# Update passes: where VectorE does the second and the third head's scan and product around the edge layer norm

## What is computed

```python
for i in range(L):                       # L = 3, H = 4 heads, dh = 16
    q, k, v = h @ Wq[i], h @ Wk[i], h @ Wv[i]      # per head
    scores = einsum('ehd,ehd->eh', q[dst], k[src]) / sqrt(dh)
    scores = scores + e @ We[i]
    p = exp(scores - segment_max(scores, dst)[dst])
    alpha = p / (segment_sum(p, dst)[dst] + 1e-09)
    agg = segment_sum(alpha[:, :, None] * v[src], dst)
    h = ln(h + agg @ Wo[i])
    emsg = gelu(concat([h[src], h[dst], e]) @ Wem[i] + bem[i])
    e = ln(e + emsg)                     # 32 features an edge
```

## Time and profile before

| | us |
|---|---|
| median of 3 runs | 10914.1 (10911.99 to 10914.28) |
| profiled execution | 10918.62 |
| its span, first to last instruction | 10916.8 |
| VectorE busy in the span | 6547.4 (60%) |
| POOL busy | 8001.4 (73%) |
| PE busy | 5191.6 (48%) |
| ScalarE busy | 4657.7 (43%) |

### The profile page before, as it was taken

The page is one execution under the profiler, slowest core; times in us unless marked ns, Lnnn a source line. Parts: engine busy times, 40 slices in busy tenths (PEclk is TensorE's granted clock), DMA queues, the critical chain, the costliest instruction groups (busy, mean ns, idle before and its releaser), DMA issues. The chain is left out here.

```text
span 10916.8 us, 87549 instructions
## 1 busy us (share of the span) xinstructions
PE 5191.6 (48%) x22037; PEld 4373.7 (40%) x22037; DVE 6547.4 (60%) x11572; ACT 4657.7 (43%) x5207; POOL 8001.4 (73%) x7864
## 2 busy tenths in 40 slices
PE   5344426885885786688588400011111433343333
PEld 5333425774774676577477300011111322232222
DVE  6333325664665566566466555554555688858887
ACT  0010004664664665566466322223333455535553
POOL 7888885776776776777677677767776777757774
PEclk8555556996997898799699655555555566656665
DMA  5333333332332232233254333333443555535553
GB/s 191 34 34 38 34 21 87 81 82 49 83 79 64 67 81 72 58 81 82 62 135 129 103 113 120 121 92 126 133 131 110 162 176 183 176 116 177 184 175 103
DMA packets 693316, 1131.52 MB, mean 104 GB/s; under 512 B 403255, under 2 KB 468070, under 8 KB 685558
## 3 DMA queue, kind: packets, MB, share of 16 engines
q0 software_dynamic: 364224, 383.74, 18.7%
q1 hardware_dynamic: 265088, 397.86, 11.4%
q10 hardware_dynamic: 63926, 349.09, 8.1%
HBM read 674.29 MB, written 468.68 MB: 105 GB/s over the span
## 5 line engine op out<-in xcount | busy, mean ns | idle before, releaser
L877 POOL DMA_INDIRECT turned<-d_t,idx x6076 | 5749.1, 946 | 1921.6 <-issue 1851.3
L1032 PE MATMUL banks<-pair,hot 128*128 128x462 f32 x13720 | 3177.7, 395 | 680.0 <-DVE wide L1127 586.0
L1032 PEld LDWEIGHTS banks<-pair,hot 128*128 128x128 f32 x13720 | 2759.3, 203 | 1097.5 <-DVE wide L1127 678.3
L648 POOL DMA_INDIRECT d_acc<-work,idx x784 | 1237.9, 1579 | 252.0 <-issue 234.4
L1237 DVE COPY idx<-src 128x28 int32 x252 | 45.8, 182 | 1871.5 <-DMA turned<-d_t,idx 1868.8
L1325 DVE TENSOR_TENSOR_SCAN wide<-banks,wide 128x224 f32<-128x224 f32 (+1 forms) x1008 | 1023.7, 1077 | 6.0 <-DVE wide L1319 0.3
L930 ACT ACTIVATE hot<-wide,row 128x896 fp32r<-128x896 f32 x980 | 930.1, 1030 | 77.7 <-DMA wide<-d_key 48.9
L1064 PE MATMUL banks<-ident,wide 128*128 128x128 f32 x588 | 162.0, 421 | 1681.3 <-ACT wide L897 863.2
L1305 DVE TENSOR_TENSOR wide<-turned,banks 128x1792 f32<-128x1792 f32 x252 | 860.3, 3414 | 0.0
L1003 ACT COPY wide<-wide 128x924 f32<-128x924 f32 (+1 forms) x252 | 477.2, 1894 | 873.2 <-DVE wide L1325 869.3
L1064 PEld LDWEIGHTS banks<-ident,wide 128*128 128x128 f32 x588 | 102.3, 211 | 1748.8 <-ACT wide L897 894.4
(11 more groups left out here) (295 smaller groups left out, 8308.5 us busy)
## 6 DMA issues: line engine op xcount, KB each, us to landing
d_e<-wide ACTq DMA_DIRECT2D x168, 924.0 KB
turned<-d_t,idx POOLq DMA_INDIRECT x6076
d_e<-wide ACTq DMA_DIRECT2D x84, 1008.0 KB
wide<-d_b SPq DMA_DIRECT2D x60, 1344.0 KB
wide<-d_key SPq DMA_DIRECT2D x145, 448.0 KB, 3.7
wide<-d_b SPq DMA_DIRECT2D x60, 896.0 KB, 4.6
d_b<-wide SPq DMA_DIRECT2D x28, 1344.0 KB
wide<-d_edge SPq DMA_DIRECT2D x84, 448.0 KB, 5.3
```

The costliest lines, as they stand in the source:

```text
L648: gp.indirect_dma_start(g.d_acc[r][:, :], offset(idx[:, b, k:k + 1]), sums[:, b, k, :], None, compute_op=ALU.add).then_inc(added[b][r], 16)
L877: gp.indirect_dma_start(rows[:, b, k, :], None, table[:, :], offset(idx[:, b, k:k + 1])).then_inc(s["gathered"][b], 16)
L1032: mm = nc.tensor.matmul(ps_cols[i], hot[:, place, i, j, :], flat(g.pair[:, part, j]), start=(j, part) == (0, 0), stop=(j, part) == (SETS - ...
```

## The change

In update passes, the scan and product of head 2 and the product of head 1 change their places among VectorE's instructions:

- before the layer norm stood product 0, scan 1, product 1, scan 2; now product 0, scan 1
- in the wait for ScalarE's squares stood product 2; now product 1
- behind the layer norm stood scan 3, product 3; now scan 2, product 2, scan 3, product 3.

```diff
@@ -1240,15 +1240,13 @@
                 e = e_rows[:, b]
                 link(product_q(G, 0))
                 link(spread_q(b, 1))
-                link(product_q(G, 1))
-                link(spread_q(b, 2))
                 v.wait_ge(s["gelu_done"], chunk + 1)
                 v.wait_ge(s["e_loaded"][b], 16 * (t + 1))
                 link(nc.vector.tensor_tensor(norm, norm, e, ALU.add))
                 link(nc.vector.tensor_reduce(stat[:, 0], norm, AX.X, ALU.add))
                 nc.vector.scalar_tensor_tensor(norm, bc(stat[:, 0], DE), -1.0 / DE, norm,
                                                ALU.mult, ALU.add).then_inc(s["centred"], 1)
-                link(product_q(G, 2))
+                link(product_q(G, 1))
                 v.wait_ge(s["squared"], chunk + 1)
                 link(nc.vector.tensor_reduce(stat[:, 1], sq[:], AX.X, ALU.add))
...
@@ -1264,7 +1262,7 @@
             else:
-                for i in range(0 if not update else 3, NH):
+                for i in range(0 if not update else 2, NH):
                     if i:
                         spread = spread_q(b, i)
                         if i == NH - 1:
```

## The result

| | before | after |
|---|---|---|
| median of the runs, us | 10914.1 (10910.6 to 10914.7) | 10855.5 (10854.4 to 10858.7) |
| profiled execution, us | 10918.62 | 10855.53 |
| its span, us | 10916.8 | 10853.6 |
| mean granted clock of TensorE | 0.688 | 0.691 |

The ratio is 0.9948, with a 95% interval from 0.9934 to 0.9962: 58.6 us less, where 54 were forecast. In the listing of after the lines of the update pass stand two lower: L1245 is the norm's first add (before L1247), L1258 the new e, L1285 the addition to the logits, L1303 the weighting of v.

What follows compares the result with a forecast made beforehand. VectorE's work before the norm set its start, the gelu lying ready 1.42 or 0.86 us. Twice 27.9 is 55.8, less 2 for gathers: 54 off 10918.62 gives 10864.6; the median's 4.5 lower gives 10860, range 10842 to 10880.

Steps and rivals of the forecast that it cites:

- The wait at L1287 is cover, and the gelu is the limit: Update chunks: L1287's wait covers the moved 1.92 us, falling from 149.8 to about 42; gelu ready only 1.42 or 0.86 early.
- 13 x 1.32 + 14 x 0.76 a pass: Front of the norm: gain per chunk of each kind after a 0.1 us hand-over; with 0.1 for chunk 0, 27.9 us.
- The gathers at the start of a pass: Chunk 3 of the second pass: late gathers lose about 1.1 us once; 2 us taken for both passes, between 0 and 6.
- POOL: Gathers need 35.06 us a chunk against 35.4: POOL stops waiting in most chunks, stays behind for some 18 each pass.
- 0.3 us to spare behind the new e: Before L1287: VectorE ready 15.1 us after t, L1287 at t + 15.40 in the quickest chunks, so all moved work is covered.
- The squares' wait: Sum behind the squares: product of head 1 replaces that of head 2, same shape, 0.44 us stays open, nothing changes.
- The table load: Ahead of the gelu: rows give 2.21 us from L1005; the skill's drain would give 2.66, some 12 us less gain.
- (a): Rival, TensorE's clock at the We product: all chunks slow 10869, all quick 10842; chance 0.82 together with the forecast.
- (b): Rival: the gelu waits for PE's sums (L1082) at the low clock, 41 us of gain lost, 10901; chance 0.05.
- (c): Rival, no gain: a wait the trace does not show eats the 1 us a chunk, 10914; chance 0.07.
- (d): Rival, slower: gathers' landing decides above 9.5 us, makes it slower above 11.5; 10921, or 10948 with one more; chance 0.05.
- (e): Rival: the whole 1.92 us a chunk taken from in front of the norm is won, 10807; chance 0.01.

Runs made afterwards that it cites:

- scan-only kernel: Against the changed kernel, the product of head 1 went back in front of the norm, nothing filling the squares' wait: 10855.86 us, ratio 0.9948.
- pair on one chip: The changed kernel and the kernel before, each run again unchanged with a profile on the same chip: 10858.24 us and 10912.74 us.
- more work behind the new e: Against the changed kernel, scan 1 went into the wait for the squares and product 1 behind the new e: 10858.66 us, ratio 0.9951.
- before with ReLU: The kernel before with ReLU in place of the edge gelu, results not the reference's: 14158.88 us, ratio to before 1.0012.
- all eight kernels: ReLU in before and in the changed kernel; on the changed kernel gelu early twice, exponentials early twice, both, both with 26 gathers: 13876.36 to 14158.88 us.
- kernels with the exponentials early: Changed kernel with ScalarE's message-row copy (L912) and store moved behind the exponentials: 14097.79 and 14004.84 us; with the gelu early too: 14026.92.
- early gelu: Changed kernel with the next chunk's gelu issued between ScalarE's two state copies: 14141.04 us and again 14060.24, ratios 0.9998 and 0.9988 to before.
- two gathers fewer: Changed kernel with gelu and exponentials early, POOL gathering 26 of 28 columns, results not the reference's: 13876.36 us, ratio 0.9861 to before.

## Why the prediction was right

**The wait at L1287 is cover, and the gelu is the limit.** Right. The wait ends at t + 16.02 whatever VectorE does, before and after, and went from 149.8 to 41.6 us, with 42 forecast. The chunk lost 1.0 us and not the 1.92 that left the front. The scan-only kernel shows it most directly: 1.25 us taken out of the front do as much as 1.92.

**13 x 1.32 + 14 x 0.76 a pass.** The total came out near (for both passes 55.8 forecast, 54 with the gathers' 2 us off; 52.0 and 54.0 measured in two pairs of profiles), with two terms off that partly cancel: this one and the gathers'. The hand-over from the gelu to the first add was taken as 0.10 us throughout. It is 9000.77 - 9000.58 = 0.19 in one kind of chunk and 9851.73 - 9851.64 = 0.09 in the other (rows below). At 13 or 14 chunks a pass this costs 1.3 us a pass, inside the bound of 0 and 0.2 that stood beside it. The idle time in front of the add, forecast as 1.2 and 0.6, is 1.18 and 0.82 in the chunks shown. Of the 0.2 us in the second kind, 0.09 are the hand-over, and 0.13 are only counting: before, too, the add started 0.13 us behind the end of the scan pair (9022.20 + 1.15 to 9023.48), and the row of after counts from that end.

**The gathers at the start of a pass.** 2 us were taken off, 0 were lost. Chunk 3 of the second pass in after, on PE, ScalarE and VectorE:

```profile
9848.42 1.77 PE L1082 MATMUL banks<-turned,ident 128*128 128x512 f32 x4 [0.99 <-DMA turned<-d_t,idx]
```
```profile
9849.45 1.28 ACT L967 ACT_TABLE_LOAD   x1 [0.53 <-ACT wide L1005]
9850.74 0.90 ACT L967 ACTIVATE banks<-banks 128x896 f32<-128x896 f32 x1
```
```profile
9851.73 1.10 DVE L1245 TENSOR_TENSOR banks<-banks,wide 128x896 f32<-128x896 f32 x1 [1.18 <-issue]
```

The add comes 9851.73 - 9745.53 = 106.2 us behind the first one, 3 x 35.4: no gather was late. The forecast had taken the gathers' landing from the kernel before, L1082 at 9887.52 - 9783.04 = 104.48 behind the first add. In after it starts at 9848.42 - 9745.53 = 102.89. POOL issued the chunk's last gather at the same place:

```profile
9881.27 1.00 POOL L877 DMA_INDIRECT turned<-d_t,idx  x1 [0.30 <-issue]
```
```profile
9843.67 0.95 POOL L877 DMA_INDIRECT turned<-d_t,idx  x1 [0.30 <-issue]
```

The first is of before, 98.23 behind the first add, the second of after, 98.14 behind. So the gathers landed 5.25 us behind the end of the last issue before and 3.80 us behind it after. The pair on one chip shows the same, L1082 at 104.64 and at 102.79. With the old landing PE's sums would have ended at 104.48 + 1.77 = 106.25 and the add would have come 1.0 us late, as forecast. What failed is taking the landing as fixed, and why it is shorter in the changed kernel is open.

**POOL.** Right: its waits for the weighting of v beyond the usual 0.30 went from 35.5 - 24 x 0.30 = 28.3 us in the first pass to 4.4 - 8 x 0.30 = 2.0, and 1.4 more that the view puts under "issue". Where POOL waits for it, a group starts 0.81 us behind its end. This is first so at the 18th chunk of the first pass and the 14th of the second, where the forecast had some 18 for each.

**0.3 us to spare behind the new e.** Right as a row: the quickest chunks leave 0.23 to 0.28 us. Wrong as a margin. The prediction treated L1287 as the point where lateness starts to cost. With more work behind the new e the wait in front of it was used up, and 0.4 us were lost in the medians and 2.3 in the passes of the two profiles, where this reading, carried into the expectation of that run, gave 12. The wait of up to 1.2 us behind it is in the profile of before as well:

```profile
DVE wide L1304 <- ACT first_f L987: 63.9, 56, 1.2
```

It had been taken for a part of the line from the logits to the weighting of v. But what releases it comes from ScalarE's own line.

**The squares' wait.** Unchanged, 0.44 before and 0.45 after, as forecast. And the scan-only kernel adds that filling it is worth nothing while the gelu sets the start of the norm.

**The table load.** The forecast went by the row. After the change the last copy ends at 8997.46, the load takes 1.28 us from 8998.38, and the gelu starts at 8999.68, 0.02 us behind it: 2.22 us from copy to gelu, as before the change, and not 2.66. The Trainium skill (ScalarE: Activation LUTs, What ACT_TABLE_LOAD costs) is right on the load's 1283 ns; its drain of about 1380 ns for each switch has no room here, where the engine stood free for 0.92 us already. Nor is there room where ScalarE is busy up to the load: in the lines of the kernel with more work behind the new e, L901 ends at 8988.28, the load starts at 8988.30, and the next instruction starts at 8989.59, 0.01 us behind the load.

**Rivals.** (a) The clock did not move: 0.62 and 0.63 in the passes before, 0.63 and 0.63 after, with both lengths of L1285's wait mixed as ever. (b) The gelu waits for ScalarE's own load in all chunks but the first of a pass; PE's sums come last there, and end 0.32 us or more ahead of the gelu in all others. (c) The moved scans did not slow each other or the turning of e: 9.33 and 16.02 stand. (d) Landing never decided, though PE now stands for gathers more often: beside the first chunk of each pass in 15 chunks, 18.6 us, where it was 5 and 6.8 us. (e) The gelu forbade it.

**The level.** 10860 was the forecast and 10855.5 the median. Between the profiled executions there are 63.1 us, of which 10.0 lie in code ahead of the passes and 7.4 of those belong to the execution or the chip. So the nearness of 10860 to 10855.5 says less than the 54 us of the passes do.

## What to carry to other kernels

Before work is moved into a wait, ask what the engine will wait for next at the place that it leaves: a wait may be 2.7 us long and the gain 1.0, because the partner's result lies ready by only that much. And the length of a wait is not yet the cover that it gives; where the next wait on the same engine is ended by a partner that does not need this engine's late result, that second wait is cover too, up to what the partner takes. Compare two executions of an unchanged stretch before a difference in it is put to an edit.

## What the runs showed that was not expected

**POOL's pitch differs between executions of one program.** In the passes ahead of the update passes POOL issues without a stop: from 1900 to 2500 us 479 gathers, 452.9 us busy and 148.9 us of the usual idle time between two. 8585.70 against 8578.33 us for the same program is a difference of 0.09%, and between the profiles of before and after the lead grows evenly along those passes: 1.3 us at 1794, 4.8 at 4472, 9.9 at 8545. On the one chip POOL's first gather of the first update pass is at 8537.43 in the kernel before, at 8535.63 and 8535.82 in the changed kernel and the scan-only one, and at 8540.29 in the one with more work behind the new e. A few microseconds of a difference of two profiles can come from it.

**On two of the chips all kernels took 13.9 to 14.2 ms instead of 10.9.** The kernel before had medians of 14142.38 us (14086.59 to 14177.98) on the one and 14074.08 (14022.79 to 14126.52) on the other. The trace of before with ReLU shows where (waits in the whole span):

```profile
DVE wide L1127 <- remote: 2205.5, 160, 35.5
PE banks L1032 <- issue: 2073.0, 1144, 4.9
...
ACT we_rows L908 <- remote: 1341.8, 79, 36.7
```

In the update passes, ScalarE's copy of the We product starts some 11 us late:

```profile
11512.12 3.08 PE L1100 MATMUL banks<-w_cat,wide 128*128 128x144 f32 x14
...
11520.92 0.95 POOL L877 DMA_INDIRECT turned<-d_t,idx  x1 [0.30 <-issue]
11526.19 0.38 ACT L908 COPY we_rows<-banks 128x48 f32<-128x48 f32 x3 [13.34 <-remote]
...
11534.49 0.94 POOL L877 DMA_INDIRECT turned<-d_t,idx  x1 [12.61 <-DVE wide L1305]
```

PE's records end at 11515.2 and ScalarE, which needs nothing else there, starts at 11526.19, released by something that the profile does not name. The instructions take what they take elsewhere, a matmul of the We product 435 ns against 434 and a gather 947 ns against 944 and 946; the engines stand still between them. The mean granted clock is 0.636 against 0.688.

The wait has an order that is the same in the traces of all eight kernels. The copy starts 4.2 to 5.0 us behind the end of POOL's last gather of the group under way (here 11526.19 - 11521.87 = 4.32), in all but two of the chunks with the long wait. The first gather of the next group starts 8.3 us behind the copy's start (11534.49 - 11526.19), and 7.4 us in the kernels with the exponentials early. So the gathers and the line from the We copy to the weighting of v take turns, 34.7 + 4.4 + 8.3 = 47.4 us a chunk, and the chunks of before with ReLU are 46.6 and 48.3 us long in turn. On the chips of 10.9 ms the copy waits for PE's We product (155.4 us in 56 chunks before), and the gathers run beside it.

This tells what these chips can show. The gelu's end lies in none of the three terms, so neither ReLU nor an early gelu moves the chunk. Early exponentials shorten the third, and two gathers fewer the first. Why the copy comes only behind the gathers there is not shown by these runs.
